# Moving the indexer of a sparse attention into layer 0 of a transformer kernel, with one activation table for Exp and Ln and later zeroing

## What is computed

```
xn = layernorm(x)
s  = sparse_latent_attention(xn)      # 8 heads, top 96 keys per query, 64 of them the local window
g  = silu(two_layer_ffn_net(xn))      # 2 layers: local attention (window 64) and a gated feed-forward
out = x + s * g

# the indexer inside the sparse attention: which 32 far keys a query takes
q_i = xn @ idx_wq   (4 heads of 64);  k_i = xn @ idx_wk
I   = sum_h idx_w[h] * relu(q_i[h] . k_i)          # per query and key
idx = top_k(I with the local window at +inf and the future at -inf, 96)

# one layer of the second branch (twice)
q, k, v = shift(x) @ wqkv;  q, k = l2norm, scale, rotate
x = x + softmax(local(q, k)) v @ wo
h = layernorm(shift(x));  a, g = h @ w1 + b1;  x = x + (a * gelu(g)) @ w2 + b2
```

## Time and profile before

| | |
|---|---|
| median of 3 runs | 1639.14 us (1638.55 to 1643.65) |
| the profiled execution's own time | 1635.37 us |
| its span, first to last instruction | 1633.7 us |
| mean granted TensorE clock in it | 0.828 of full |
| busy: TensorE matmul, VectorE, ScalarE, GpSimd | 71%, 61%, 38%, 15% of the span |

### The profile page before, as it was taken

How to read it: one execution, slowest core, us unless ns; L and a number is a source line. 1 busy time by engine, 2 the same in 40 slices (tenths; PEclk the granted TensorE clock), 3 DMA queues, 4 the chain that set the end, 5 groups by cost and what they waited for, 6 DMA issues and landing times. The chain is left out here.

```text
span 1633.7 us, 22979 instructions
## 1 busy us (share of the span) xinstructions
PE 1154.4 (71%) x8816; PEld 755.5 (46%) x8816; DVE 992.6 (61%) x1835; ACT 623.1 (38%) x1381; POOL 251.6 (15%) x172
## 2 busy tenths in 40 slices
PE   2777876578497777569749687756856868684785
PEld 2454542456255354146526445325643545532563
DVE  2575856676356574767527567386842948637773
ACT  0352445233225354524322525543332442553332
POOL 0320302001122131101012122120001302111000
PEclk9998975789689898579959889857977989866897
DMA  5000001553000000165200000026410000005530
GB/s 212 1 1 1 1 1 52 94 78 48 5 1 1 1 1 15 39 110 77 32 5 1 1 0 2 14 71 98 72 19 4 1 1 1 1 14 106 90 55 10
DMA packets 231276, 54.51 MB, mean 33 GB/s; under 512 B 220048, under 2 KB 230800, under 8 KB 230800
## 3 DMA queue, kind: packets, MB, share of 16 engines
q1 hardware_dynamic: 231152, 52.86, 17.8%
HBM read 45.37 MB, written 7.47 MB: 32 GB/s over the span
## 5 line engine op out<-in xcount | busy, mean ns | idle before, releaser
L1129 PE MATMUL PS<-onehot,CX 128*96 128x512 bf16 x320 | 91.9, 422 | 93.5 <-DVE onehot L1358 90.6
L1381 DVE TENSOR_REDUCE xnT<-PS 32x64 f32<-32x192 f32 x256 | 90.8, 355 | 69.2 <-ACT V L1307 65.6
L579 ACT ACTIVATE S<-S,nbias,rnorm 128x128 f32<-128x128 f32 x256 | 122.3, 479 | 25.8 <-DVE nbias L735 25.8
L1299 ACT ACTIVATE KC<-PS 96x1024 bf16<-96x1024 f32 x64 | 65.1, 1018 | 126.2 <-PE PS L1129 126.2
L1358 DVE TENSOR_SCALAR onehot<-idxb,consts 128x1024 bf16<-128x1024 f16 x160 | 77.6, 537 | 52.9 <-DMA idxb<-idx_scratch 48.7
L566 ACT ACTIVATE sq<-PS 128x512 f32<-128x512 f32 x64 | 38.2, 597 | 178.1 <-PE PS L376 178.1
L1135 PEld LDWEIGHTS PS<-onehot,XR 128*96 128x96 bf16 x1280 | 87.5, 134 | 25.6 <-DVE KR L1364 16.1
L1129 PEld LDWEIGHTS PS<-onehot,CX 128*96 128x96 bf16 x320 | 36.9, 132 | 126.6 <-DVE onehot L1358 101.5
L700 DVE SCALAR_TENSOR_TENSOR pb<-PS,wts,consts 128x512 f32<-128x512 f32 x64 | 48.0, 750 | 77.0 <-PE PS L376 75.1
L1135 PE MATMUL PS<-onehot,XR 128*96 128x128 bf16 x1280 | 92.1, 232 | 3.2 <-DVE KR L1364 2.9
L1364 DVE CAST KR<-PS 96x1024 bf16<-96x1024 f32 x64 | 78.1, 1220 | 26.7 <-PE PS L1135 25.7
(11 more groups left out here) (218 smaller groups left out, 2649.9 us busy)
## 6 DMA issues: line engine op xcount, KB each, us to landing
idxb<-idx_scratch SPq DMA_DIRECT2D x64, 256.0 KB, 4.9
q3c<-q_scratch SPq DMA_DIRECT2D x96, 96.0 KB, 3.0
q3r<-q_scratch SPq DMA_DIRECT2D x96, 96.0 KB, 3.8
q_scratch<-q3s SPq DMA_DIRECT2D x16, 384.0 KB, 2.5
wts<-weights_dram SPq DMA_DIRECT2D x1, 4825.5 KB, 20.6
consts<-consts_dram SPq DMA_DIRECT2D x1, 2612.5 KB, 9.0
x_next<-x_dram SPq DMA_DIRECT2D x5, 256.0 KB, 6.5
out<-soft_kr SPq DMA_DIRECT2D x16, 64.0 KB, 1.7
```

What stands on the lines that cost most here:

```text
L579: last = op(S[:, i, h, :], S[:, i, h, :], ACT.Exp, bias=nbias[:, i, h:h + 1], scale=rnorm[:, Q, h // 2, i, h % 2:h % 2 + 1], accum_out=rsu ...
L1129: last = mm(k.Z[0:96, e, :], k.CX[:, j, :], onehot[:, n % 2, j, e * 512:(e + 1) * 512], start=(j == 0), stop=(j == i))
L1299: op(KC[:, i % 2, :, :].rearrange("p t (g r) -> p t g r", g=GR)[:, :, :, q * RB:(q + 1) * RB], k.Z[0:96, :, :].rearrange("p a (r g t) -> p ...
L1381: last = ve.tensor_reduce(SN[32 * g:32 * g + 32, :, 8 * o:8 * o + 8].rearrange("p h t -> p t h"), part, AX.X, ALU.add)
```

## The change

1. In `project`, the matmuls of the indexer's queries and keys and its scores become functions (`index_queries`, `index_keys`, `index_scores`). In layer 0 the first two are called behind `values(l, 3)`, ahead of `prob_T(l, 0)`, queries first; `index_scores(i)` is called behind `weigh_values(l, i)`. TensorE's wait for `zeroed` moves ahead of layer 0's scores.
2. ScalarE's copies of them (`index_copies`) go behind the last tile's Exps of layer 0; the ReLUs of tile i (`relus`) behind `copy_pT` i + 1.
3. VectorE's picks: those of tile 0 leave layer 0's projections. Head sums and the first two picks go into layer 0's attention behind `copy_o` 1 and 2; the other two, the conversion and tile 1's head sums go behind the feed-forward's token shift; tile 1's picks follow behind hn and the products. Layer 1 keeps its picks of tiles 2 and 3 where they were.
4. ScalarE loads the table `natural_log_exp_and_others` behind `norms(l, Q)` of both layers and at the start of `latents`.
5. GpSimd waits for all four `xn` tiles before it zeroes.

The diff, cut (the bodies of moved functions are the same as before):

```diff
@@ TensorE, project
-            pe.wait_ge(a.xnT_ready, 1)
-            rY.start(pe, "ki", a.ki_ready, 1)
-            mm(k.Y[:, 0, :], W("idxk2"), k.xnT[:, WIN:], start=True, stop=True).then_inc(rY.full, 1)
-            rX.start(pe, "qi", a.qi_ready, 1)
-            for c in range(2):
-                last = mm(k.X[:, c, :], W("idxq", c * P, P), k.xnT[:, WIN:], start=True, stop=True)
-            last.then_inc(rX.full, 1)
-            pe.wait_ge(a.zeroed, 1)
-            pe.wait_ge(a.ki_ready, 1)
-            pe.wait_ge(a.qi_ready, 1)
-            for i in range(TILES):
+            def index_queries():
...
+            def index_keys():
...
+            def index_scores(i):
+                if i == 0:
+                    pe.wait_ge(a.ki_ready, 1)
+                    pe.wait_ge(a.qi_ready, 1)
                 for hp in range(2):
...
                 pe.wait_ge(a.k_ready, PAIRS * (l + 1))
+                if l == 0:
+                    pe.wait_ge(a.zeroed, 1)
...
                 values(l, 3)
+                if l == 0:
+                    index_queries()
+                    index_keys()
                 prob_T(l, 0)
                 for i in range(TILES):
                     if i + 1 < TILES:
                         prob_T(l, i + 1)
                     weigh_values(l, i)
+                    if l == 0:
+                        index_scores(i)
                     if i:
                         project_heads(l, i - 1)
@@ GpSimd, project
+            pool.wait_ge(a.xn_ready, TILES)
             for par in range(2):
                 nc.gpsimd.memset(kiZ[half(1 - par), par, :], 0.0)
@@ ScalarE, project
+            def index_copies():
+                act.wait_ge(rX.full, rX.nth("qi"))
+                op(qiT[:, :, :], k.X, ACT.Copy).then_inc(a.qi_ready, 1)
+                act.wait_ge(rY.full, rY.nth("ki"))
+                act.wait_ge(a.zeroed, 1)
+                for par in range(2):
+                    last = op(kiZ[half(par), par, :], k.Y[half(par), 0, :], ACT.Copy)
+                last.then_inc(a.ki_ready, 1)
...
                 norms(l, Q)
+                nc.scalar.preload_act_table_set("natural_log_exp_and_others")
                 copy_v(l, 0)
                 for i in range(TILES - 1):
                     exps(l, i)
                 copy_pT(l, 0)
                 exps(l, TILES - 1)
+                if l == 0:
+                    index_copies()
                 for i in range(1, TILES):
                     copy_pT(l, i)
+                    if l == 0:
+                        relus(i - 1)
+                if l == 0:
+                    relus(TILES - 1)
@@ VectorE, project
-                    if n == 0:
-                        sum_heads(2 * l)
-                    if n in (1, 2, 3):
-                        next_best(2 * l, n - 1)
-                    if n == 5:
-                        next_best(2 * l, 3)
-                    if n == 6:
-                        keep_indices(2 * l)
+                    if l:
...
+                if l == 0:
+                    copy_o(l, 0)
+                    copy_o(l, 1)
+                    sum_heads(0)
+                    copy_o(l, 2)
+                    next_best(0, 0)
+                    next_best(0, 1)
+                    copy_o(l, 3)
+                else:
...
                 shift_tokens(x1, 1)
-                next_best(2 * l + 1, 3)
-                keep_indices(2 * l + 1)
+                if l == 0:
+                    next_best(0, 2)
+                    next_best(0, 3)
+                    keep_indices(0)
+                    sum_heads(1)
+                else:
...
                 ve.tensor_tensor(hn, k.X[:, 0, :], rn, ALU.mult).then_inc(a.hn_ready, 1)
+                if l == 0:
+                    next_best(1, 0)
+                    next_best(1, 1)
                 for j, (o, n) in enumerate(HCH):
...
+                    if l == 0 and j < 2:
+                        next_best(1, 2 + j)
+                if l == 0:
+                    keep_indices(1)
```

More of the change, by code:

```diff
@@ L349, in _ @@
             last.then_inc(rZ.full, 1)
-            pe.wait_ge(a.xnT_ready, 1)
-            rY.start(pe, "ki", a.ki_ready, 1)
-            mm(k.Y[:, 0, :], W("idxk2"), k.xnT[:, WIN:], start=True, stop=True).then_inc(rY.full, 1)
-            rX.start(pe, "qi", a.qi_ready, 1)
-            for c in range(2):
-                last = mm(k.X[:, c, :], W("idxq", c * P, P), k.xnT[:, WIN:], start=True, stop=True)
-            last.then_inc(rX.full, 1)
-            pe.wait_ge(a.zeroed, 1)
-            pe.wait_ge(a.ki_ready, 1)
-            pe.wait_ge(a.qi_ready, 1)
-            for i in range(TILES):
+            def index_queries():
+                rX.start(pe, "qi", a.qi_ready, 1)
+                for c in range(2):
+                    last = mm(k.X[:, c, :], W("idxq", c * P, P), k.xnT[:, WIN:], start=True, stop=True)
+                last.then_inc(rX.full, 1)
+            def index_keys():
+                rY.start(pe, "ki", a.ki_ready, 1)
+                mm(k.Y[:, 0, :], W("idxk2"), k.xnT[:, WIN:], start=True, stop=True).then_inc(rY.full, 1)
+            def index_scores(i):
+                if i == 0:
+                    pe.wait_ge(a.ki_ready, 1)
+                    pe.wait_ge(a.qi_ready, 1)
                 for hp in range(2):
@@ L542, in _, with relus @@
             op(k.xnT[:, WIN:], k.Z[:, 0, :], ACT.Copy).then_inc(a.xnT_ready, 1)
-            act.wait_ge(rY.full, rY.nth("ki"))
-            act.wait_ge(a.zeroed, 1)
-            for par in range(2):
-                last = op(kiZ[half(par), par, :], k.Y[half(par), 0, :], ACT.Copy)
-            last.then_inc(a.ki_ready, 1)
-            act.wait_ge(rX.full, rX.nth("qi"))
-            op(qiT[:, :, :], k.X, ACT.Copy).then_inc(a.qi_ready, 1)
-            for i in range(TILES):
+            def index_copies():
[6 more added lines that the diff above has]
+                last.then_inc(a.ki_ready, 1)
+            def relus(i):
                 for hp in range(2):
@@ L757, in _ @@
                     parts(l, n)
-                    if n == 0:
-                        sum_heads(2 * l)
-                    if n in (1, 2, 3):
-                        next_best(2 * l, n - 1)
-                    if n == 5:
-                        next_best(2 * l, 3)
-                    if n == 6:
-                        keep_indices(2 * l)
+                    if l:
+                        if n == 0:
+                            sum_heads(2)
+                        if n in (1, 2, 3):
+                            next_best(2, n - 1)
+                        if n == 5:
+                            next_best(2, 3)
+                        if n == 6:
+                            keep_indices(2)
                     if n == PAIRS:
@@ L783, in _ @@
                 recips(l, 3)
-                sum_heads(2 * l + 1)
-                copy_o(l, 0)
-                next_best(2 * l + 1, 0)
-                copy_o(l, 1)
-                next_best(2 * l + 1, 1)
-                copy_o(l, 2)
-                next_best(2 * l + 1, 2)
-                copy_o(l, 3)
+                if l == 0:
[7 more added lines that the diff above has]
+                else:
+                    sum_heads(3)
+                    copy_o(l, 0)
+                    next_best(3, 0)
+                    copy_o(l, 1)
+                    next_best(3, 1)
+                    copy_o(l, 2)
+                    next_best(3, 2)
+                    copy_o(l, 3)
                 dve.wait_ge(rU.full, rU.nth(f"wo{l}.{TILES - 1}"))
@@ L795, in _ @@
                 shift_tokens(x1, 1)
-                next_best(2 * l + 1, 3)
-                keep_indices(2 * l + 1)
+                if l == 0:
[4 more added lines that the diff above has]
+                else:
+                    next_best(3, 3)
+                    keep_indices(3)
                 if l == LAYERS - 1:
```

## The result

The changed kernel takes **1585.66 us** (median of four executions, 1576.22 to 1593.44) beside 1638.85 us for the kernel before on the same chip: a ratio of 0.9678, interval 0.9601 to 0.9755, 53 us less. The forecast was 1597 us in a range of 1577 to 1614. The profiled execution of the changed kernel took 1576.22 us, the fastest of the four; that of the kernel before took 1635.4 us.

The account below looks back on a forecast made before the run. No engine is full; one chain repeats four times, its last wait differing by stage. Front -59.3, clock +10.6, projections -11.6, attention +30.4 and tables -12.4 sum to -42.3: 1597 us from 1639.1; 80% lie in 1577 to 1614.

Parts of the forecast that it names:

- The front: Norms to first projection matmul: indexer leaves, zeroing waits for the norms, projections start when hT is ready; -59.3 us together.
- Rival 3: Front: the second hT copy loses its turn and waits out a further big memset, 2.1 us each; 1605 us, chance 0.10.
- Clock and projections: Layer 0's projections: start at 1.2 GHz, +10.6 us; without tile 0's picks scores start 2.9 us sooner, -11.6 us.
- The cold start: Layer 0's projections start at 1.2 GHz; 5.3 us at half clock do 2.65 us of work, +10.6 over four elements.
- Attention: Layer 0's attention takes in the indexer's matmuls, copies and scores: 7.6 us an element, +30.4; bounds 2 and 23.5.
- the forecast's queue: TensorE's order of work in layer 0's attention, timed from the first score matmul: last projects end at 45.2, now 37.35.
- Rivals 1: Layer 0's attention: indexer work falls into TensorE's idle time and costs 2 us, not 7.6; 1575 us, chance 0.08.
- 2 (+23.5 an element): Layer 0's attention: TensorE and ScalarE in lockstep at 1.2 GHz, projects end at 60.9; 1660 us, chance 0.04.
- Feed-forward of layer 0: Picks of tiles 0 and 1 on VectorE fit the waits at no cost; up to 1 us an element otherwise.
- Tables: One table for Exp and Ln: loads leave both layer norms and layer 1's softplus; 3.1 us an element, -12.4.
- Rival 4: The preload does not hold: a load for Exp is put in again, none in a chain goes; 1609 us, chance 0.05.
- Sum: Adds the terms, -59.3 + 10.6 - 11.6 + 30.4 - 12.4 = -42.3, taken from the median of 1639.1: 1597 us.

Follow-up runs that it names:

- again: The changed kernel run once more with no edit, in a second profiled execution of 1585.17 us; its median was 1584.69 us, ratio 0.9684.

## Why the prediction was right, and where it was off

**The front: right.** hT 7.08 us instead of the forecast 7.2, the first projection matmul right behind, -57.45 for -57.5 us. Rival 3 (the second copy loses its turn) happened in none of four elements. The Trainium skill's rule on VectorE copies and GpSimd (SBUF — State Buffer, Who interferes with whom) spoke against the edit, and the runs bear it out: held, the first copy takes 1.63 us, with GpSimd silent 0.42; the edit as made is worth nothing that the whole time shows, and the place behind hT 1.28 us an element in the front and 12 us in the whole.

**Clock and projections: right.** 27.08 us without picks (forecast 26.95). The cold start, the changed kernel's sum less that of the picks alone, is 118.13 - 108.33 = 9.8 us (forecast 10.6): 3.0, 2.5 and 2.8 us in elements two to four and 1.5 in the first, whose wide matmuls go at the slow pace (1.06 us each) for only 2.7 us.

**Attention: the mechanism right, the term mis-sized.** This is the step that failed most: +30.4 forecast, +24.4 (or +23.7 in "again") measured. In the second element the forecast's queue holds to within a microsecond: index 0 starts at 25.04 (forecast 25.45), index 1 at 30.55 (31.1), index 3 at 39.31 (40.2), the end comes at 44.37 (45.2). But I took that element for all. Elements one and four of the kernel before needed 38.30 and 38.27 us, not 37.35, which is 1.9 us of the miss, and elements one and three of the changed kernel end at 43.50 and 43.57, with some 3.5 instead of 7 us at 1.2 GHz, another 1.6. The rest, 0.6 to 0.7 us an element, is the queue itself, a little slow at each tile. Rivals 1 (+2) and 2 (+23.5 an element) are out; ReLUs were no tile's releaser.

**Feed-forward of layer 0: right as far as the picks go.** They cost the feed-forward nothing: with the same picks the stage takes 9.66 us when warm. That it grew by 2.3 us in sum goes with the clock: elements one and four took 11.29 us at a granted clock of 0.85 and now take 12.39 and 12.23 at 0.74 and 0.75, as the other two did before (12.25). Ahead of hn the picks fit with 0.88 us to spare, as forecast, but only while part of the wait is cold; where it is warm they are the last to end, by 0.1 us.

**Tables: the loads as forecast, their worth not.** -1.28 and -1.87 us an element are what the waits for hn show at about equal clock (8.48 to 7.20, 9.00 to 7.13), for a forecast of 1.28 and 1.83. But the preloads were worth 18 to 25 us by the medians, not 12.4, and a wait of plain copies cost as much. Rival 4 is out. The step that was missing is in "Sum": it added stages as if the ones not edited kept their time. They did not: the same 18 matmuls of layer 1's feed-forward took 9.59 us at a granted clock of 1.00 and 12.30 at 0.74, and the forecast has no term for that, nor a width.

Together: forecast -42.3, "again" -50.7 by its stages, of which the attention is 6.7; the stages set at nothing make 5.2, the remaining terms give 3.5 back. In the fastest execution the stages set at nothing make 11. Both misses go the same way, and that their sum still lies in the range is partly luck, since nothing in the forecast sized the second.

**What stays open**: what decides between layer 1's warm and cold forms in the kernels whose wait is not filled. The changed kernel shows both in one execution; with the tables alone no feed-forward is warm, though one wait is (6.18 us). It shows already in layer 1's attention (39.4 or 40.6 us). Open too is what sets attend's time, which shifts by more than some of the edits are worth.

## What to carry to other kernels

Where an engine's granted clock moves, as TensorE's does here between 0.74 and 1.00 over the same matmuls, cost an edit twice: by its path, and by what it does to idle times ahead of dense stages elsewhere; and give the sum a term, or at least a width, for stages that nobody edits. Useful work of the same engine, put into its longest waits, can be worth more than its own length (here 3 us of index scores an element brought nearly 5). Take a stage's length from all its repetitions before extrapolating from one.

## What the runs showed of the hardware beyond expectation

One program in one execution ran the same 18 matmuls in 9.59 or 12.30 us, depending on a granted clock of 1.00 or 0.74. Ahead of either case TensorE had mostly waited: 3.14 us busy of 7.13 ahead of the slow one, partly cold itself, and 2.20 of 6.18 ahead of the fast one. So the wait alone does not decide it. With two more matmuls in that wait (3.05 us busy of 6.18), whose results nobody reads, all four elements had the fast case. The Trainium skill (TensorE: Matmul & The Clock Gate, HAM oscillation — how this bites in real kernels) describes the clock falling in repeated waits between groups of matmuls; the cold elements agree (0.72 in the wait, 0.74 behind it), and the warm ones of the same execution show that an equal wait can also pass at 1.00. And 1.3 us more of ScalarE's time in that wait, by a table load or by two copies alike, cost 23 to 25 us by the medians where 10 to 13 were added; the surplus is in part the cold form of layer 1 in all four elements, and in part attend's, which stays open.
